# A wavelet mixing kernel: the identity taken away inside the accumulation, and half of the block diagonal operand built by ScalarE

## What is computed

```python
yl, yh = _dwt2(x, _LEVEL)
yl_out = jnp.einsum('bixy,ioxy->boxy', yl, w_yl)
yh_out = yh[:-1] + [jnp.einsum('bicxy,iocxy->bocxy', yh[-1], w_yh)]
return _idwt2(yl_out, yh_out)
```

## Time and profile before

| | us |
|---|---|
| median of 3 runs | 2210.77 (2210.68 to 2211.38) |
| span of the profiled execution | 2209.3 |
| analysis, until the last transposes | about 0 to 770 |
| mixing, from the first copy into `diag` | 768.5 to 906.4 |
| synthesis | 906.5 to 2209.3 |

### The profile page before, as it was taken

How to read it: one execution, slowest core, us unless ns; L and a number is a source line. 1 busy time by engine, 2 the same in 40 slices (tenths; PEclk the granted TensorE clock), 3 DMA queues, 4 the chain that set the end, 5 groups by cost and what they waited for, 6 DMA issues and landing times.

```text
span 2209.3 us, 30374 instructions
## 1 busy us (share of the span) xinstructions
PE 1991.7 (90%) x10288; PEld 830.3 (38%) x10288; DVE 942.7 (43%) x1723; ACT 443.7 (20%) x1007; POOL 3.6 (0%) x7
## 2 busy tenths in 40 slices
PE   8999999999999944799989889889889889889886
PEld 3344343443434334444433333333333333333332
DVE  2222222222222399655544444444444444444443
ACT  2222222222222211212112112112112112112110
POOL 0000000000000000000000000000000000000000
PEclk9999999999999955899999999999999999999998
DMA  9999999999999776599999999999999999999999
GB/s 383 408 363 353 363 342 370 345 363 353 346 363 350 266 263 226 169 387 404 408 409 409 409 409 409 409 409 409 409 409 409 408 409 409 409 409 409 409 408 386
DMA packets 406628, 827.08 MB, mean 374 GB/s; under 512 B 12752, under 2 KB 13520, under 8 KB 406608
## 3 DMA queue, kind: packets, MB, share of 16 engines
q1 hardware_dynamic: 406608, 826.80, 99.6%
HBM read 558.32 MB, written 268.44 MB: 374 GB/s over the span
## 4 chain that ended last, share of the span: by engine, by line
DMA 46%; PE 42%; SPq 5%; issue 4%; DVE 3%; DVEq 0%; ACT 0%; ACTq 0%
DMA out<-x_sb 45%; PE ps L327 21%; PE ps L337 7%; PE ps L349 5%; PE ps L451 5%; SPq L278 5%; DVE both L642 2%; PE ps L441 1%; DMA x_sb<-x 1%; PE ps L365 1%; PE ps L407 1%; DVE both L647 0%; PE ps L431 0%; SPq L273 0%; DVEq L642 0%
## 5 line engine op out<-in xcount | busy, mean ns | idle before, releaser
L451 PE MATMUL ps<-spread,const 128*128 128x512 f32 x2048 | 941.0, 602 | 112.4 <-DVE x_sb L671 112.4
L671 DVE TENSOR_TENSOR x_sb<-ps,x_sb 128x1024 f32<-128x1024 f32 x500 | 592.0, 1220 | 670.1 <-DMA x_sb<-x 598.9
L451 PEld LDWEIGHTS ps<-spread,const 128*128 128x128 f32 x2048 | 372.3, 189 | 680.8 <-issue 401.4
L327 PE MATMUL ps<-x_sb,const 128*64 128x512 f32 x2048 | 494.3, 604 | 8.7 <-DMA x_sb<-x 8.7
L570 ACT COPY spread<-ps 84x512 f32<-84x512 f32 x256 | 148.8, 581 | 970.7 <-PE ps L441 970.3
L621 DVE COPY work<-ps 128x80 f32<-128x80 f32 x256 | 61.8, 241 | 560.3 <-PE ps L337 560.3
L441 PE MATMUL ps<-const,pick 128*84 128x512 f32 x512 | 261.3, 592 | 0.7 <-issue 0.7
L490 ACT COPY work<-ps 128x512 f32<-128x512 f32 x256 | 150.0, 586 | 537.5 <-PE ps L327 537.5
L327 PEld LDWEIGHTS ps<-x_sb,const 128*64 128x64 f32 x2048 | 129.8, 136 | 205.3 <-issue 189.2
L337 PEld LDWEIGHTS ps<-const,work 128*128 128x128 f32 x1024 | 107.0, 140 | 207.6 <-issue 206.1
L337 PE MATMUL ps<-const,work 128*128 128x128 f32 x1024 | 167.7, 286 | 0.4 <-ACT work L490 0.3
(11 more groups left out here) (20 smaller groups left out, 219.4 us busy)
## 6 DMA issues: line engine op xcount, KB each, us to landing
x_sb<-x SPq DMA_DIRECT2D x498, 1024.0 KB, 12.6
out<-x_sb SPq DMA_DIRECT2D x250, 1024.0 KB, 13.2
both<-w_full SPq DMA_DIRECT2D x30, 896.0 KB, 4.7
work<-x SPq DMA_DIRECT2D x6, 1024.0 KB, 9.3
out<-work SPq DMA_DIRECT2D x6, 1024.0 KB, 12.8
both<-w_rest SPq DMA_DIRECT2D x6, 224.0 KB, 2.5
const<-consts SPq DMA_DIRECT2D x1, 912.0 KB, 4.7
```

The costliest lines, as they stand in the source:

```text
L327: last = nc.tensor.matmul(ps[64 * j:64 * j + 64, p], const[:, AH + 64 * k:AH + 64 * k + 64], x_sb[:, c, k], start=k % 2 == 0, stop=k % 2 == 1)
L451: last = nc.tensor.matmul(ps[:, 2 + k], const[:, SH + P * k:SH + P * k + P], spread[:, p], start=True, stop=True)
L671: nc.vector.tensor_tensor(part, ps[:, 2 + 2 * half:4 + 2 * half], part, ALU.add).then_inc(added[half], 1)
```

## The change

DVE no longer touches the weights. PE begins each part with one matmul for each line, minus the identity against all 448 columns of that line's `diag`, with start=True and stop=False. The 56 weight matmuls follow with start=False and accumulate on it. PE now waits for the weights themselves (`w_loaded`), behind these first matmuls. The copies into `diag` are split: DVE makes those of q = 0 and 1 (`build_low`), ACT those of q = 2 and 3 (`build_high`), for part c+2 right behind `copy_mixed` of part c. `diag_built` and `w_ready` give way to `low_built` and `high_built`. The order of the DMAs on SP is the same.

```diff
-                pe.wait_ge(diag_built[a], PARTS // 2 * v + c // 2 + 1)
-                pe.wait_ge(w_ready[wb], PARTS // WBUFS * v + c // WBUFS + 1)
+                pe.wait_ge(low_built[a], PARTS // 2 * v + c // 2 + 1)
+                pe.wait_ge(high_built[a], PARTS // 2 * v + c // 2 + 1)
                 pe.wait_ge(mixed_copied[a], PARTS // 2 * v + c // 2 + 1)
+                for l in range(n):
+                    nc.tensor.matmul(ps[32 * l:32 * l + 32, a, 0:U * QB], const[:, NEG:NEG + CHANNELS],
+                                     diag[:, a, l].rearrange("p u n -> p (u n)"), start=True, stop=False)
+                pe.wait_ge(w_loaded[wb], 16 * (PARTS // WBUFS * v + c // WBUFS + 1))
                 for u in range(U):
                     for l in range(n):
                         last = nc.tensor.matmul(ps[32 * l:32 * l + 32, a, QB * u:QB * u + QB],
-                                                w[:, u, l], diag[:, a, l, u], start=True, stop=True)
+                                                w[:, u, l], diag[:, a, l, u], start=False, stop=u == U - 1)
                 last.then_inc(mixed[a], 1)
...
+            def build_high(c, v, n):
+
+                a = c % 2
+                act.wait_ge(mixed[a], PARTS // 2 * v + c // 2 + 1)
+                for q in range(Q // 2, Q):
+                    part = slice(32 * q, 32 * q + 32)
+                    src = mix_sb[part, v, :, 0:n, U * c:U * c + U].rearrange("p b l u -> p l u b")
+                    last = nc.scalar.copy(diag[part, a, 0:n, :, BATCH * q:BATCH * (q + 1)], src)
+                last.then_inc(high_built[a], 1)
...
-            with act.Fori(0, FULL) as v:
+            act.wait_ge(diag_cleared, 1)
+            act.wait_ge(m_copied, STEPS * BATCH)
+            build_high(0, 0, 4)
+            build_high(1, 0, 4)
+            with act.Fori(0, FULL - 1) as v:
                 for c in range(PARTS):
                     copy_mixed(c, v, 4)
+                    build_high((c + 2) % PARTS, v + (c + 2) // PARTS, 4)
+            for c in range(PARTS):
+                copy_mixed(c, FULL - 1, 4)
+                after = FULL - 1 + (c + 2) // PARTS
+                build_high((c + 2) % PARTS, after, lines(after))
             for c in range(PARTS):
                 copy_mixed(c, FULL, lines(FULL))
+                if c + 2 < PARTS:
+                    build_high(c + 2, FULL, lines(FULL))
...
-            def build(c, v, n):
-
-                a, wb = c % 2, c % WBUFS
+            def build_low(c, v, n):
+
+                a = c % 2
                 dve.wait_ge(mixed[a], PARTS // 2 * v + c // 2 + 1)
-                for q in range(Q):
+                for q in range(Q // 2):
                     part = slice(32 * q, 32 * q + 32)
                     src = mix_sb[part, v, :, 0:n, U * c:U * c + U].rearrange("p b l u -> p l u b")
                     last = nc.vector.tensor_copy(diag[part, a, 0:n, :, BATCH * q:BATCH * (q + 1)], src)
-                last.then_inc(diag_built[a], 1)
-                dve.wait_ge(w_loaded[wb], 16 * (PARTS // WBUFS * v + c // WBUFS + 1))
-                w = w_sb[:, wb, 0:U * n * CHANNELS].rearrange("p (k o) -> p k o", o=CHANNELS)
-                minus_eye = const[:, NEG:NEG + CHANNELS].rearrange("p (k o) -> p k o", k=1)
-                nc.vector.tensor_tensor(w, w, minus_eye.to_broadcast([P, U * n, CHANNELS]),
-                                        ALU.add).then_inc(w_ready[wb], 1)
+                last.then_inc(low_built[a], 1)
```

More of the change, by code:

```diff
@@ L194, in wavelet_mix_kernel @@
         w_loaded = sems("w_loaded", WBUFS)
-        w_ready = sems("w_ready", WBUFS)
-        diag_built = sems("diag_built", 2)
+        low_built = sems("low_built", 2)
+        high_built = sems("high_built", 2)
         mixed = sems("mixed", 2)
@@ L642, in build @@
                     last = nc.vector.tensor_copy(diag[part, a, 0:n, :, BATCH * q:BATCH * (q + 1)], src)
-                last.then_inc(diag_built[a], 1)
-                dve.wait_ge(w_loaded[wb], 16 * (PARTS // WBUFS * v + c // WBUFS + 1))
-                w = w_sb[:, wb, 0:U * n * CHANNELS].rearrange("p (k o) -> p k o", o=CHANNELS)
-                minus_eye = const[:, NEG:NEG + CHANNELS].rearrange("p (k o) -> p k o", k=1)
-                nc.vector.tensor_tensor(w, w, minus_eye.to_broadcast([P, U * n, CHANNELS]),
-                                        ALU.add).then_inc(w_ready[wb], 1)
+                last.then_inc(low_built[a], 1)
             dve.wait_ge(diag_cleared, 1)
-            dve.wait_ge(const_loaded, 16)
             with dve.Fori(0, FULL) as v:
@@ L654, in _ @@
                 for c in range(PARTS):
-                    build(c, v, 4)
+                    build_low(c, v, 4)
             dve.wait_ge(m_copied, STEPS * BATCH)
             for c in range(PARTS):
-                build(c, FULL, lines(FULL))
+                build_low(c, FULL, lines(FULL))
             for a in range(2):
```

## The result

The changed kernel takes **2176.02 us** (median of 4 runs, 2174.81 to 2177.28) against 2211.07 for the kernel before on the same chips (2210.68 to 2213.59): a ratio of 0.9838, 95% interval 0.9825 to 0.9851, or 35 us less. The prediction was 2170, range 2161 to 2195. The profiled span fell from 2209.3 to 2174.7 us.

A forecast was written before the change was run, and what follows sets the result against it. DVE was taken to bound the mixing at 4.15 us a part. Gains of +4 and 23 x (4.15 - 2.4) = +40.2, less 0.7, 1.2 and 1.5, gave 41 us, so 2170, range 2161 to 2195.

The forecast's parts named there:

- +4 and -1.5: First round: 4 us gained up to the seventh copy back, and 1.5 us lost until the clock has risen.
- The new matmuls and the clock: Full part on PE: identity matmuls 0.8 us, weight matmuls 1.1, 1.6 in all; clock rises to 2.4 GHz and stays.
- rival C: The wide identity matmuls of four groups run one after another: 4.1 us a full part, 2220 in all; chance 0.07.
- rival B: PE clock in mixing stays at or falls back to 1.2 GHz: 17 to 24 us gained, 2187 to 2194; chance 0.19.
- ScalarE's copy: ACT's new copies into `diag`: 0.57 us each, 1.7 us a part for two with the copy back.
- the ring: Two buffers turning between PE and ACT: 1.9 us a part at full clock, 2.6 at half, hidden under 2.4 or 3.0.
- The load term: Weight loads of a full part become the bound at full clock: 2.4 us (382 GB/s), bounds 2.24 and 2.7.
- The floor: Least time for a full part's weight load: 917,504 bytes at 409 GB/s, 2.24 us.
- listed signs: Signs in the new trace: copies back 2.4 us apart, L541 at 0.57, DMA 370 to 409 GB/s, PEclk near 1.0.
- The first round: Up to the seventh copy back: 5 fetch holes of 2.4 us plus 6 parts of 1.6; 4 us gained.
- The small parts: Six parts after the full ones: 0.7 us more in all, and 1.2 more for an x load queued ahead.
- Rival D: Program text is fetched on every pass of the loop: 3.6 us a part, about 2200 in all; chance 0.06.

The follow-up runs named there:

- e2: The changed kernel, but VectorE takes the identity from the weights as before while ScalarE builds half of the operand: 2191.42 us, ratio 0.9906.
- e8: The changed kernel with three of the four copies on VectorE and one on ScalarE: 2177.47 us, ratio 0.9844.
- e1: The changed kernel with all four copies on VectorE, TensorE still taking the identity away: 2178.50 us, ratio 0.9849.
- e12: The changed kernel with the last four early loads of x (1 MB each) issued behind the last weights: 2169.46 us, ratio 0.9808.
- e6: The changed kernel with TensorE's loop over the five full rounds written out, so all its program text is new: 2206.79 us in one run.
- e9: The changed kernel with ScalarE's two copies unlike, one with strided reads and straight writes, one the reverse (output differs): 2179.06 us in one run.
- e7: Four copies on VectorE in the changed kernel, and weights laid out so loads move pieces of 1792 bytes, not 7168: 2178.70 us, ratio 0.9843.
- e11: The changed kernel with three copies on VectorE and the early loads of x behind the weights: 2169.61 us, ratio 0.9809.
- e3: The changed kernel with ScalarE's two copies reading 14 floats in a row and writing 32 floats apart: 2176.32 us, ratio 0.9854.

## Why the prediction was right, and where its steps were off

**The direction and the place** were right. DVE's 4.15 us were the bound, the gain lies in the 23 steady parts (36.6 us; 40.2 forecast), and the synthesis moved as a block (1303.4 and 1302.0 us). The measured 2176 is 6 us over the forecast and inside the range. The 6 us are 3.6 in the steady parts (2.557 us each for 2.4), 2.9 up to the 7th copy back (0.4 later, where the sum had 2.5 earlier, +4 and -1.5), 1.1 in the small parts, less 1.4 in the synthesis.

**The new matmuls and the clock** were right. Eight records of 448 columns took 0.96 us, 0.15 more than the low end of 0.81, and by no means the 3.24 of rival C. The 112 records took 1.16, where 1.1 was taken. The clock was at 2.4 GHz in all steady parts, with PE busy 0.78 of the time, so rival B did not come. In e2, where PE was busy 0.52, it stayed at 1.2.

**ScalarE's copy is the first step that was mis-sized**: 0.57 us was taken, 0.97 measured. The step scaled two ACT copies by their element count and did not ask how they walk through memory: L548 of before reads 336 floats in a row, the new copy reads 336 floats apart. ScalarE's part so became 2.53 and not 1.7, longer than the 2.4 of the load that was to hide it. The prediction's bound "if the copies took 1.0 us each, the ring would be 2.3 and still hide" counted the ring and forgot ACT's own sum, 0.54 + 2 x 0.97 + 0.05 = 2.53, which is larger.

**The load term is the second**: 2.4 us (382 GB/s) was taken, and e8 and e1 show 2.58 to 2.68. The best steady stretch with full loads is e12's 2.53, paced by ScalarE, so 2.4 was reached nowhere. The floor was worked out from 409 GB/s, a rate of the synthesis, where half the bytes are stores. Where the kernel before only loads, its trace had a nearer number, and the prediction gave such slices as its upper bound only:

```profile
200.00:300.00 100.00, 100.00 (x533) 40.06 (x531) 26.45 (x136) 24.74 (x48) 0.00 (x0) 1.00 1.01 357
```

917,504 bytes at 357 GB/s are 2.57 us. By either term the forecast would have been 23 x 0.14 to 0.17 = 3 to 4 us higher; the two errors are of about the same size, so that mending only one of them would have given the same number.

**The bound that took over** was named as the DMA alone. It is ScalarE in most of the steady parts and the loads in some, and in e12 ScalarE alone. That the number came out near is therefore in part luck: the overlooked ScalarE term happened to be only 0.13 us over the load term that was taken. Three of the listed signs stood off: copies back 2.54 us apart and not 2.4, L541 at 0.97 and not 0.57, and the DMA at 352 GB/s and not 370 to 409.

**The first round** was forecast 4 us shorter up to its end and was 0.4 longer. The holes stand where they were said to (each 128 records) and are what they were said to be (e6). The two longest took 3.4 and 4.6 us and not 2.4, but the four that can be seen (3.35, 4.63, 1.68 and 0.51) add up to 10.2 us, less than the 12 taken. What failed is the work between them. The sum counted six parts, 9.6 us, where seven lie ahead of the 7th copy back, and all at full clock, where PE was at 1.2 GHz for some 13 of the 28.6 us from its first matmul to that copy. It was busy 17.6 us of them. PE also began at 773.15, not 772.0, as ACT's copies were slower.

**The small parts** cost 3.0 us more, where 1.9 was taken; the first wait for `w_rest` behind the early load of x was 1.5 (without that load, in e12, the small parts cost 0.9 more than before, near the 0.7 forecast):

```profile
863.00 1.07 PE L411 MATMUL ps<-both 128*32 128x32 f32 x28 [1.54 <-DMA both<-w_rest]
```

**Rival D**, text fetched on every pass, did not come: from the second round on most parts of the looped kernel take 2.52 to 2.55 us, queue 8 has no packet between 802 and 860 us, and e6 shows what such parts would look like.

## What to carry to other kernels

When an engine that bounded a loop is relieved, sum up every other engine's own work for one turn and the bytes of one turn at a rate taken from a stretch with the same mix of loads and stores; here two such sums (2.53 for ScalarE, 2.57 for the loads at 357 GB/s) lay side by side, so that ScalarE's half of the change, and a remedy for either one alone, brought little or nothing. Scale a copy from one that walks through memory in the same way, not from one with the same number of elements. Look for transfers that are issued at the stage's start, where new program text is fetched too: moving 4 MB of loads to a slack stretch brought 9 us, a quarter of what the change itself brought, half of it in the first round.

## What the runs showed of the hardware that was not expected

- An ACT copy of 32x448 fp32 within SBUF takes 0.56 us when it reads in a row and 0.96 when it reads 336 floats apart (e9). DVE's copies with the same strided read took 0.54 (L667, two in 1.08).
- Four matmuls of 448 columns in four column groups, 8 records, take 0.96 us at 2.4 GHz. The 112 weight records take 1.16 at 2.4 GHz and 1.73 at 1.2, not twice as much.
- Pure loads went at 350 to 363 GB/s with a DMA share of 0.96 to 1.01 (e8, the analysis of the kernel before, e12), loads and stores together at 409.
- Loads come unevenly once nothing paces them: with three buffers parts of 1.7 to 4.4 us stood side by side (e1, e7, e8, e11), at a mean of 2.58 to 2.79. Paced by ScalarE the same loads gave even parts of 2.52 to 2.58 (e12, e3). Why is open; the length of the pieces is not it (e7), and more buffers were not tried.
- PE stops for program text once in 128 records where that text is new. The longest stop of the first round was 2.6 us without the loads of x in the queue (e12), and 4.6 and 5.1 with them (the changed kernel, e1); the shortest that can be seen took 0.2 and 0.5.
